# The turned context and the turned-back context exchange their PSUM banks in a two-layer gated attention kernel

## The reference

```python
x = x + tanh(g_xattn[0]) * L0_xattn(_layernorm(x), ctx, ctx, mask, ...)   # masked, 16 heads of 8
x = x + tanh(g_ffn[0])   * L0_ffn(_layernorm(x), ...)                     # 8 experts, top 2, plus a shared one
x = x + tanh(g_xattn[1]) * L1_xattn(_layernorm(x), ctx, ...)              # no mask
x = x + tanh(g_ffn[1])   * L1_ffn(_layernorm(x), ...)                     # token shift, sigmoid gate, squared relu
# attention: scores = q k / sqrt(8); ctx = softmax(scores) v; out = ctx Wo + bo
```

## Time and profile before

| | us |
|---|---|
| median of 3 runs | 323.95 |
| lowest, highest | 319.15, 324.38 |
| the profiled execution | 319.62 |
| its span, first to last instruction | 317.3 |
| mean granted TensorE clock | 0.928 |

### The profile page before, as it was taken

One profiled execution on the slowest core, in us unless ns is written; L12 is line 12 of the kernel. 1 busy time (PEld: TensorE's weight loads), 2 busy tenths in 40 slices (PEclk: granted clock), 3 DMA queues, 4 the chain that ended last, 5 costly groups with the idle time before them and its releaser, 6 DMA issues.

```text
span 317.3 us, 7826 instructions
## 1 busy us (share of the span) xinstructions
PE 262.6 (83%) x2904; PEld 194.2 (61%) x2904; DVE 203.7 (64%) x645; ACT 184.6 (58%) x376; POOL 91.3 (29%) x161
## 2 busy tenths in 40 slices
PE   0813979999999999887997988989898869799870
PEld 0301656677678778654574756866766758679550
DVE  2320576676677687684458356876866946997980
ACT  1411345978987886985664455177677634676330
POOL 3410052143142341301101012322613512731460
PEclk9965796999999999999999999979999975999995
DMA  8457446744443443000000251444454452000121
GB/s 221 114 172 193 130 124 174 194 141 126 122 132 108 122 119 101 6 0 2 0 2 0 80 169 25 120 126 125 126 161 115 127 156 61 6 5 2 33 66 33
DMA packets 27677, 30.45 MB, mean 96 GB/s; under 512 B 13715, under 2 KB 24820, under 8 KB 26484
## 3 DMA queue, kind: packets, MB, share of 16 engines
q1 hardware_dynamic: 20446, 27.12, 29.3%
q10 hardware_dynamic: 4188, 2.47, 3.1%
q0 software_dynamic: 3008, 0.39, 0.8%
HBM read 22.43 MB, written 7.14 MB: 93 GB/s over the span
## 4 chain that ended last, share of the span: by engine, by line
PE 59%; DVE 13%; DMA 8%; issue 6%; POOL 5%; ACT 4%; ACTq 1%; SPq 1%; DVEq 0%; POOLq 0%
PE bank L1266 9%; PE bank L1227 8%; PE bank L1201 6%; PE bank L1363 5%; PE bank L1197 4%; DMA QS<-qparts 3%; DMA QS<-nmT 3%; DVE nmx L520 3%; PE bank L1166 3%; PE bank L1293 2%; PE bank L1223 2%; PE bank L1156 2%; PE bank L1143 2%; PE bank L1311 2%; PE bank L1275 2%
## 5 line engine op out<-in xcount | busy, mean ns | idle before, releaser
L520 DVE TENSOR_REDUCE nmx<-bank 128x4 f32<-128x480 f32 x128 | 82.9, 653 | 58.4 <-PE bank L1201 57.2
L411 POOL DMA_DIRECT2D QS<-nmT x94 | 46.4, 499 | 139.5 <-ACT nmT L931 139.3
L940 ACT ACTIVATE P<-bank 120x512 f32<-120x512 f32 x128 | 75.3, 592 | 18.4 <-PE bank L1227 17.2
L1227 PE MATMUL bank<-QS,KS 75*120 75x128 bf16 x512 | 53.6, 229 | 2.6 <-DMA QS<-nmT 1.6
L1201 PE MATMUL bank<-KS,QS 72*128 72x120 bf16 x512 | 51.0, 224 | 2.6 <-issue 2.6
L1201 PEld LDWEIGHTS bank<-KS,QS 72*128 72x128 bf16 x512 | 40.2, 102 | 20.8 <-issue 10.5
L1227 PEld LDWEIGHTS bank<-QS,KS 75*120 75x120 bf16 x512 | 43.7, 139 | 10.1 <-ACT P L940 2.4
L1266 PE MATMUL bank<-P,VS 120*32 120x128 f32 x1024 | 36.2, 284 | 5.4 <-DVE cn L555 4.3
L1266 PEld LDWEIGHTS bank<-P,VS 120*32 120x32 f32 x1024 | 27.5, 113 | 9.0 <-ACT P L940 4.9
L1197 PE MATMUL bank<-MB,IDH 128*128 128x480 bf16 x64 | 25.1, 392 | 5.3 <-DMA QS<-qparts 4.0
L907 ACT ACTIVATE kp<-bank,BC 128x480 bf16<-128x480 f32 x23 | 15.1, 658 | 19.5 <-PE bank L1143 11.8
(11 more groups left out here) (138 smaller groups left out, 437.1 us busy)
## 6 DMA issues: line engine op xcount, KB each, us to landing
KS<-kparts SPq DMA_DIRECT2D x48, 180.0 KB
QS<-qparts SPq DMA_DIRECT2D x42, 192.0 KB
kparts<-kp SPq DMA_DIRECT2D x24, 120.0 KB, 3.5
qparts<-qp SPq DMA_DIRECT2D x21, 128.0 KB, 3.4
QS<-nmT POOLq DMA_DIRECT2D x94, 4.0 KB, 2.2
QS<-qparts ACTq DMA_DIRECT2D x6, 192.0 KB
X<-in_x SPq DMA_DIRECT2D x3, 256.0 KB, 14.4
out<-X SPq DMA_DIRECT2D x3, 256.0 KB, 2.3
```

Source lines behind the costliest of these rows:

```text
L411: po.dma_start(QS[G % 2][STACK + p:STACK + p + 1, k // 2, :, (k % 2) * S:(k % 2 + 1) * S], nmT[Bi % 2][p * H:(p + 1) * H, :]).then_inc(m_l ...
L520: ins = nc.vector.tensor_reduce(nmx[Bi % 2][:, UH * r:UH * r + UH], QS_BANK[U % 3][:, 0:UH * SK].rearrange("p (h k) -> p h k", k=SK), AX.X ...
L940: nc.scalar.activation(P[Bi % 2][:, hh, :], src, ACT.Exp, scale=SCALE).then_inc(exp_done, 1)
L1227: last = mm(o[0:SK, j * S:(j + 1) * S], KS[G % 2][0:ROWS, k // 2, h, (k % 2) * SK:(k % 2 + 1) * SK], QS[G % 2][0:ROWS, k // 2, h, (k % 2) ...
```

## The change

`turn_back` writes to bank 5, columns 256 to 511, up to Bi = B+10, and to bank 4 as before from B+11. `turn_ctx` writes to bank 4, columns 256 to 383, up to Bi = B+9, and to bank 5 as before from B+10. The readers (`cn` on VectorE, `ct_copy` on ScalarE) follow. The waits are set anew: `values(Bi)` waits for `ct_copy(Bi-2)` in place of `cn(Bi-1)` up to B+11; `turn_max` waits for `cn(Bi-4)` in place of `ct_copy(Bi-5)`; `turn_back` also waits for `nt_copy(Bi+3)` and `cn(Bi-1)`; `turn_ctx` no longer waits for `nt_copy` up to B+9; the first `moe_out` waits for the last `ct_copy` of layer 0 in place of the last `cn`. The order of the instructions on every engine stays.

```diff
+        def back_bank(Bi):
+            return (bank[5] if Bi < B + 11 else bank[4])[:, 2 * S:4 * S]
+        def ctx_bank(Bi):
+            return bank[4][:, 2 * S:3 * S] if Bi < B + 10 else bank[5][:, 0:S]
...
-                    pv = bank[4][:, 2 * S:4 * S].rearrange("p (h c) -> p h c", c=CW)
+                    pv = back_bank(Bn).rearrange("p (h c) -> p h c", c=CW)
...
-                nc.scalar.activation(cT[Bi % 2][:, :], bank[5][:, 0:128], ACT.Copy).then_inc(ct_evac, 1)
+                nc.scalar.activation(cT[Bi % 2][:, :], ctx_bank(Bi), ACT.Copy).then_inc(ct_evac, 1)
...
             def turn_max(Bi):
-                if Bi % B >= 5:
-                    pe.wait_ge(ct_evac, Bi - 4)
+                if Bi % B >= 4:
+                    pe.wait_ge(cn_ok, Bi - 3)
...
             def values(Bi):
                 pe.wait_ge(exp_done, UNITS * (Bi + 1))
-                if Bi >= 1:
+                if Bi >= B + 12:
                     pe.wait_ge(cn_ok, Bi)
+                elif Bi >= 2:
+                    pe.wait_ge(ct_evac, Bi - 1)
...
             def turn_back(Bi):
                 pe.wait_ge(cx_ok, Bi + 1)
+                if Bi < B + 11:
+                    pe.wait_ge(nt_evac, min(Bi + 4, B * (Bi // B + 1)))
+                    if Bi >= 1:
+                        pe.wait_ge(cn_ok, Bi)
                 for i in range(2):
-                    last = nc.tensor.transpose(bank[4][:, (2 + i) * S:(3 + i) * S], cx[Bi % 2][:, i * S:(i + 1) * S], IDF[:, :])
+                    last = nc.tensor.transpose(back_bank(Bi)[:, i * S:(i + 1) * S], cx[Bi % 2][:, i * S:(i + 1) * S], IDF[:, :])
...
             def turn_ctx(Bi):
                 pe.wait_ge(cn_ok, Bi + 1)
-                pe.wait_ge(nt_evac, min(Bi + 5, B * (Bi // B + 1)))
+                if Bi >= B + 10:
+                    pe.wait_ge(nt_evac, min(Bi + 5, NB))
...
-                nc.tensor.transpose(bank[5][:, 0:128], cn[Bi % 2][:, :], IDF[:, :]).then_inc(ct_done, 1)
+                nc.tensor.transpose(ctx_bank(Bi), cn[Bi % 2][:, :], IDF[:, :]).then_inc(ct_done, 1)
...
             def moe_out(g, i):
                     if g == 0:
-                        pe.wait_ge(cn_ok, B)
+                        pe.wait_ge(ct_evac, B)
```

## The result

The changed kernel takes 337.09 us (median of six runs, 335.06 to 342.17) beside 321.57 us for the kernel before in the same session (six runs, 318.83 to 326.46). The ratio is 1.0508, interval 1.0442 to 1.0574: slower by 5.1%, where 2.2% was forecast, and 337 lies above the range given. Two further sessions with the same kernel gave 1.0507 (1.0417 to 1.0596) and 1.0364 (1.025 to 1.0477). So the loss to be explained is 12 to 16 us, not 6.9. Ratios compare the faster executions of each kernel (those within 1.5% of its fastest), so they differ a little from the quotient of the medians.

A forecast was written before the change was run, and what follows sets the result against it. TensorE, busy for 83% of the span, was taken to bound the kernel. 7.2 - 0.7 + 0.4 = 6.9 us took the profiled 319.62 us to 326.5 (+2.2%); the middle given was 328.7 us, the range 321.5 to 333.

The forecast's parts named there:

- Layer 0's stalls: Layer 0, values(2) to values(13): values waits for ScalarE's late copy twelve times, adding up to 7.2 us.
- three kinds: Layer 0, by what precedes the copy: fill only, 0.44 us; k_part or q_part, 0.79; XT4 copy, 0.66.
- rival B: Copy in layer 0: ScalarE late by its own backlog, only the first 0.44 us paid; 318.0 us, not slower; 9%.
- Layer 1, -0.7 us: Layer 1's values products: waits for cn removed against new waits for ScalarE's copy, about -0.7 us in all.
- ends of -2.0 and +1.1: Layer 1: -2.0 us with every gain and no loss, +1.1 us with every loss and no gain.
- It swallows what (22) and (23) do: Layer 1: the 2.61 us idle before scores_q at 258.69 absorbs values(22), -0.17 us, and values(23), +0.07 us.
- The twelve new stalls [...] too short to matter: Layer 0: stalls each under 0.9 us do not bring TensorE's clock down; only the long gap does.
- The extra waits, +0.4 us: The 27 turn_backs: an extra wait or two for TensorE's queue, +0.4 us, bounds -0.3 to +1.4 us.
- The base: One profiled execution of the kernel before, 319.62 us, at the low end of three runs; the sum was added to it.
- the step 258 to 268 us is as before: Sign of a right forecast: layer 1's step from 258 to 268 us, at low clock before, stays unchanged.
- A: Layer 1, idle before 258.69 shortens and the clock stays up: 4.0 us added, 323.6 us, within 2%; 14%.
- C: Exposed weight loads, 12 x 0.24 us, and one more low-clock stretch, 2.9 us: 12.7 us added, 332.3 us; 17%.

The follow-up runs named there:

- The earlier copy: Changed kernel with ScalarE's copy of the context moved right behind the previous step's exponential, ahead of the fill and projections' copies: 324.87 us, ratio 1.0158.
- the wait alone: Kernel before with its old banks and one wait added, values(Bi) for the copy of Bi-2: 332.82 us, ratio 1.0303.
- the later difference: Changed kernel with GpSimd's first x_difference in layer 1 one step later: 333.98 us, ratio 1.0319; the same edit with the exchange only in layer 1: 0.9989.
- layer 1 alone: Changed kernel with the new banks and waits limited to layer 1, layer 0 keeping the old ones: 326.91 us, ratio 1.0181.
- The fillers at B+8: Kernel before with 8 repeated products of 480 columns ahead of scores_q's wait for the loads at Bi = B+8: 322.02 us, ratio 0.9902.
- layer 0 alone: Changed kernel with the new banks and waits limited to layer 0, layer 1 keeping the old ones: 335.92 us, ratio 1.0328.
- the filled one with the later difference: Changed kernel with repeated products at B+8 and B+12 and GpSimd's first x_difference one step later: 328.84 us, ratio 1.0166.
- the filled one: Changed kernel with 6 repeated products of 480 columns at Bi = B+8 and 12 at B+12: 331.03 us, no ratio given.

## Why the prediction was too low

**Layer 0's stalls: right.** Twelve stalls of the three kinds were worked out by subtraction, 7.2 us. They are there, at the steps named, 0.50 to 0.53 (forecast 0.44 and 0.49), 0.81 to 0.87 (0.79), 0.72 (0.66) and 0.91 (0.85) us each: 7.96 us. What is off is mostly one small number, the time from the copy's end to TensorE: 0.11 us at nine steps and 0.07 at three, where I took 0.05 from a different pair of rows. That they add up was the point on which it hung (rival B said not): the copy ends 1.46 us after scores_k in both kernels, so a late TensorE finds it late again. The earlier copy, which takes nearly all of it away, and the wait alone, which makes them all, confirm the cause.

**Layer 1, -0.7 us: the step that failed.** The subtraction itself was sound: with the clock out of the way it is -1.6 us (-0.8 with the later difference), inside the ends of -2.0 and +1.1. But the step took each product's wait by itself and let everything else stay in step. With the exchange the maxima's DMAs are issued 0.7 us ahead of the second pair of normalises in three traces, where the old banks have them within 0.02 us of it or behind, and one normalise then ends only after GpSimd's difference. That the release from `cn` shifts them is argued from this; the shift itself was not traced step by step. About 1.5 us of VectorE's time became 1.84 us of idle on TensorE and ten microseconds at the low clock, 3 to 6 us in all by the later difference. The kernel with layer 1 alone measured +3.4 us by its medians (+5.9 by its ratio) where this step said -0.7. "It swallows what (22) and (23) do" was also said of the wrong product: the gap before 258.69 is that of scores_q of B+12 = 28, not of 24 (the values of the same step are 24). The fillers at B+8 found that out.

**"The twelve new stalls [...] too short to matter": wrong too.** The sum has no term for the clock. Through layer 0's loop this holds: the clock stays at 1.00. In the drain idles of 1.00, 0.43 and 0.87 us come within some six microseconds, and in the changed kernel (both readable traces), in layer 0 alone and in the filled one with the later difference the products behind them are at the low clock, which costs 1.55 to 1.57 us. In the wait alone, the first trace of the later difference and the filled one the clock stays up over the same idles or, in the first of these, longer ones. That is four of seven traces with these stalls, and none of the nine readable traces without them. The Trainium skill, page "TensorE: Matmul & The Clock Gate", section "A second HAM failure mode: psum-queue depth-cycling", describes short but frequent idles that bring the clock down. The four traces fit that section, the three others show that it need not happen here. The forecast cited the section on waits for data; where the line ran between the idle of 1.11 us that it took for harmless and that of 2.61 us came from two rows, and idles of 1.29 us were followed by the low clock in some traces and not in others.

**The extra waits, +0.4 us: not there.** turn_back shows no releaser but cx_copy, and with them in place but the stalls gone (the earlier copy) layer 0's loop is 0.7 us shorter than before. A wait more can still cost TensorE: 0.15 us at each of three values products in the kernel with the wait alone. No run gives a price of a wait that is long over.

**The base.** The sum was made against one execution whose layer 1 was as short as any. A second trace shows 5.6 us more for layer 1 of the same code. This doesn't change the ratio of the medians, but it made and the earlier trace rows look like the kernel, when they are one draw of it; "the step 258 to 268 us is as before" could be no test.

**The rivals.** A (the clock stays up at the gap) did not happen; the clock fell there in the changed kernel as in the one before. B fell with the stalls. C, with "one more stretch of low clock", 12.7 us, was right in kind and near in size, and it was given 17% against 60%. The nearness is in part luck: there were two such stretches (the drain and the meeting), and where I priced drained weight loads (12 x 0.24 us) only the latency above stood, 0.7 us in all.

Put together for the changed kernel: layer 0 gives 7.96 + 1.55 = 9.5 us (the kernel with layer 0 alone measured 3.28% of 325, 10.7), layer 1 the 3.4 to 5.9 us of the kernel with layer 1 alone, most of it, as far as the later difference shows, the meeting with its low clock. That is 13 to 15 us, beside 12 to 16 measured. What can't be put down to a place is the draw of the clock behind the loads' gaps, which varies by more than the rest between executions; whether the exchange makes a bad draw likelier is open.

**What stays open.** Why the clock falls in one execution and not in the next after the same idles. What exactly holds the normalise back: the ports were argued, not shown. A later place for values' wait, behind its first products, was not tried.

## What to carry to other kernels

When a wait is moved from one engine's result to another's, look at what stands in that engine's queue ahead of the result, and at what that work waits for. If the chain starts at the waiting engine itself (scores_k, exponential, fill, copy), the stall comes back at every step and the whole sum is paid; the cure is the place of the copy in the queue, which took 10 us of idle away, though even so the kernel was not faster than the one before (ratio 1.0158). A kernel whose TensorE waits for a load in mid-stage can be worth more with a few repeated products in the gap (here 2.1 to 2.5%) than with this exchange of banks. And take a second trace of the kernel before, before a stage's length goes into a sum.

## What the runs showed of the hardware

- TensorE's clock went to its 1.2 GHz level (0.50) in or behind single idles of 1.3 to 3.5 us, and after three of 1.00, 0.43 and 0.87 us close together, and it stayed there from under 4 to 38 us. The same idles did not always bring it down: one idle of 1.29 us in the middle of the feed-forward block, ahead of the same product in sixteen traces, was followed by it in four.
- A weight load of TensorE that waited for ScalarE's copy started 0.11 us after the copy's end. Where the product has a further wait it was 0.07 us, and 0.22 with one more still. In ten of the twelve stalls of layer 0 the profile names "issue" for the weight load.
- A 128x128 normalise of 0.34 us on VectorE took 1.8 us when the pair that it belongs to began 0.68 us or more after GpSimd's issues of DMAs, which a 1.05 us `tensor_tensor` follows; at 0.51 us and less it took its usual time. Started 0.07 us after a 1.28 us `tensor_tensor` of GpSimd, one took 1.29 us in every trace.
- Two executions of 1327 and 1328 us and one of 369 us turned up among over a hundred. In the trace of the first the 512 key-score products (L1235) take 704 ns each in place of 234 at a recorded clock of 1.00; the cause is unknown.
